# VectorE's scan reads its additive term from SBUF for 27 of 192 units, in a fused state-space and attention kernel

## The reference, cut to what matters

```
def step(h, inp):
    dt_t, B_t, C_t, x_t = inp
    h = jnp.exp(dt_t[:, :, None] * A) * h + (dt_t * x_t)[:, :, None] * B_t[:, None, :]
    y_t = jnp.einsum('ben,bn->be', h, C_t)
    return (h, y_t)
...
y = ys.transpose(1, 0, 2) + xr * D
y = y * jax.nn.silu(z)
return y @ W_out
```

## Time and profile before

| | |
|---|---|
| time, median of 3 runs (range) | 1211.03 us (1209.63 to 1213.32) |
| the profiled execution: its time, its span | 1210.56 us, 1208.8 us |
| DVE busy over the span | 931.2 us (77%) |
| POOL busy | 938.3 us (78%) |
| PE busy | 1055.9 us (87%) |
| ACT busy | 571.8 us (47%) |
| first read-out to last read-out of the recurrence | 58.2 to 756.6 us |

### The profile page before, as it was taken

One profiled execution on the slowest core, in us unless ns is written; L12 is line 12 of the kernel. 1 busy time (PEld: TensorE's weight loads), 2 busy tenths in 40 slices (PEclk: granted clock), 3 DMA queues, 4 the chain that ended last, 5 costly groups with the idle time before them and its releaser, 6 DMA issues. The chain is left out here.

```text
span 1208.8 us, 9466 instructions
## 1 busy us (share of the span) xinstructions
PE 1055.9 (87%) x3220; PEld 363.4 (30%) x3220; DVE 931.2 (77%) x608; ACT 571.8 (47%) x601; POOL 938.3 (78%) x375
## 2 busy tenths in 40 slices
PE   7789998789988998998878878499999999996675
PEld 2233333233332333333332223133333333332221
DVE  1499998679998999998989999400488695969871
ACT  5765867696778564866585634101111021010321
POOL 0089999989998979998999988300298977889880
PEclk9879999899999999998999999799999999998787
DMA  2244575535475545673546563253949586574402
GB/s 79 91 150 142 192 182 159 175 128 173 140 185 144 178 136 156 167 228 124 174 158 171 154 200 139 58 122 76 174 82 200 79 182 106 125 129 56 92 0 75
DMA packets 111041, 165.65 MB, mean 137 GB/s; under 512 B 63410, under 2 KB 76440, under 8 KB 110992
## 3 DMA queue, kind: packets, MB, share of 16 engines
q1 hardware_dynamic: 108880, 157.81, 50.0%
q10 hardware_dynamic: 2112, 7.23, 2.1%
HBM read 137.43 MB, written 11.23 MB: 123 GB/s over the span
## 5 line engine op out<-in xcount | busy, mean ns | idle before, releaser
L732 POOL TENSOR_TENSOR hc<-h,c_rep 128x1024 f32<-128x1024 f32 x192 | 449.6, 2354 | 99.0 <-DVE h L790 94.1
L790 DVE TENSOR_TENSOR_SCAN h<-a,bu 128x1024 f32<-128x1024 f32 x192 | 437.6, 2285 | 36.3 <-ACT bu L606 9.8
L422 PE MATMUL y_ps<-hc,ident 128*128 128x512 f32 x768 | 384.7, 626 | 3.5 <-POOL hc L732 1.9
L596 ACT ACTIVATE a<-dt,a_neg 128x1024 f32<-128x1024 f32 x192 | 216.7, 1143 | 136.5 <-DVE h L790 136.1
L1203 POOL TENSOR_TENSOR prod_p<-vw,at 128x3584 f32<-128x3584 f32 x18 | 130.2, 7236 | 122.9 <-DMA vw<-v_d 117.0
L777 DVE TENSOR_TENSOR bu<-bu,u 128x1024 f32<-128x1024 f32 x165 | 199.5, 1209 | 18.9 <-PE bu L400 18.9
L422 PEld LDWEIGHTS y_ps<-hc,ident 128*128 128x128 f32 x768 | 144.7, 197 | 213.5 <-issue 182.0
L1084 PE MATMUL sc_ps<-x,w_up 128*64 128x512 f32 x672 | 176.4, 602 | 0.0
L1084 PE MATMUL sc_ps<-x,w_low 96*64 96x512 f32 x672 | 175.7, 600 | 0.0
L400 PE MATMUL bu<-st,pick 96*128 96x512 bf16 (+1 forms) x438 | 103.1, 393 | 43.7 <-DVE h L790 40.2
L1154 ACT ACTIVATE sc<-sc_ps,rel 128x512 f32<-128x512 f32 x24 | 16.5, 687 | 246.8 <-PE sc_ps L1084 246.8
(11 more groups left out here) (126 smaller groups left out, 973.3 us busy)
## 6 DMA issues: line engine op xcount, KB each, us to landing
c_rep<-bc_d SPq DMA_DIRECT2D x128, 512.0 KB, 3.8
c_rep<-bc_d SPq DMA_DIRECT2D x128, 256.0 KB, 4.1
vw<-v_d SPq DMA_DIRECT2D x24, 532.0 KB, 9.5
x<-qk SPq DMA_DIRECT2D x66, 171.0 KB, 6.3
b_rep<-bc_d SPq DMA_DIRECT2D x17, 512.0 KB, 5.0
b_rep<-bc_d SPq DMA_DIRECT2D x20, 256.0 KB, 5.5
scores_d<-sc ACTq DMA_DIRECT2D x24, 196.0 KB
at<-scores_d SPq DMA_DIRECT2D x24, 196.0 KB, 5.1
```

What stands on the lines that cost most here:

```text
L422: mm = pe.matmul(y_ps[:, cols(th)], ident[:, :], hc[:, k % HC_RING, cols(th)], start=(n == 0 and d == 0), stop=(n == N_ST - 1))
L596: nc.scalar.activation(a[:, k % A_RING, :], dt[:, tile % 2, :], ACT.Exp, scale=a_neg[:, kind_of(tile), n:n + 1]).then_inc(exp_done, 1)
L732: nc.gpsimd.tensor_tensor(hc[:, k % HC_RING, :], h[:, k % H_RING, :], c_rep[:, k % C_RING, :], ALU.mult).then_inc(hc_done, 1)
L790: nc.vector.tensor_tensor_scan(scan_order(h[:, k % H_RING, :], d), scan_order(a[:, k % A_RING, :], d), scan_order(bu[:, k % 2, :], d), 0.0 ...
```

## The change

The 27 units of `POOL_UNITS` lose ACT's copy (`copy_b` and the semaphore `b_copied` are gone). Their scans read POOL's product where it stands, in `b_rep` in SBUF, and wait for `b_times_u`. The load that overwrites a buffer of `b_rep` waits for the scan that read it, no longer for the copy. The 165 other units are as before.

```diff
@@ SP, load_b @@
                 if i >= B_RING:
-                    sp.wait_ge(b_copied, i - B_RING + 1)
+                    sp.wait_ge(scanned, POOL_UNITS[i - B_RING] + 1)
                 replicate(b_rep, i % B_RING, k, 0, b_in[i % B_RING])
@@ ACT @@
-            def copy_b(k):
-
-                if k not in POOL_UNITS:
-                    return
-                i = POOL_UNITS.index(k)
-                act.wait_ge(b_times_u, i + 1)
-                act.wait_ge(scanned, k - 1)
-                nc.scalar.activation(bu[:, k % 2, :], b_rep[:, i % B_RING, :], ACT.Copy).then_inc(b_copied, 1)
@@
             for k in range(UNITS):
                 copy_y(k)
-                copy_b(k + 1)
                 decay(k + 2)
                 front(k)
@@ DVE, scan @@
                 if k in POOL_UNITS:
-                    dve.wait_ge(b_copied, POOL_UNITS.index(k) + 1)
+                    i = POOL_UNITS.index(k)
+                    dve.wait_ge(b_times_u, i + 1)
+                    term = b_rep[:, i % B_RING, :]
                 else:
                     dve.wait_ge(bu_done, products_before(k + 1))
+                    term = bu[:, k % 2, :]
                 if k >= H_RING:
                     dve.wait_ge(hc_done, k - H_RING + 1)
                 nc.vector.tensor_tensor_scan(
                     scan_order(h[:, k % H_RING, :], d), scan_order(a[:, k % A_RING, :], d),
-                    scan_order(bu[:, k % 2, :], d), 0.0, ALU.mult, ALU.add).then_inc(scanned, 1)
+                    scan_order(term, d), 0.0, ALU.mult, ALU.add).then_inc(scanned, 1)
```

More of the change, by code:

```diff
@@ L205, in mamba @@
         b_times_u = sem("b_times_u")
-        b_copied = sem("b_copied")
         block = ctx.enter_context(nc.Block())
```

## The result

The changed kernel takes 1269.02 us (median of 4 runs, 1267.12 to 1275.68) against 1212.17 us before: ratio 1.0481, interval 1.0438 to 1.0525, 57 us slower. The profiled execution took 1268.18 us with a span of 1266.4 us.

What follows compares the result with a forecast made beforehand. DVE and POOL together were taken to bound the recurrence, each with little slack. The terms 29.7 + 0.4 + 9 - 3 - 3 gave +33 us on 1210.56 us, 1243.6, forecast as 1244, range 1218 to 1274.

Steps and rivals of the forecast that it cites:

- the two bounds: Limits for exclusion in any order: at least +19 us (1230), and +58 (1269) if every POOL standstill arrives at the end.
- shared by halves: Rival: scan and POOL operation both run at half speed while they overlap, 59 less 3 us, 1268; chance 0.07.
- part 2: The scan's new wait for b_times_u and the load's new wait for the scan were to cost nothing.
- Alone the second operand costs hardly anything: The 27 scans' second SBUF operand, without interference, was to cost 13 ns each, 0.4 us in all.
- Exclusion, with the scan starting when POOL's operation in progress ends: The 27 scans meet POOL 94% of the time, waiting 1.10 us on average: +29.7 us; chance 0.66.
- POOL goes first: Last rival listed: DVE gets in only when POOL's queue runs dry, 3 us a scan, +81 us, 1290; chance 0.09.
- POOL loses 2.15 us a scan, 58 us in all: POOL was to stand still 2.15 us for each of the 27 scans, 1.05 us more than DVE loses each time.
- POOL's gaps swallow a part, the rest arrives as +9 us: POOL's loss beyond DVE's was to vanish in POOL's gaps; elsewhere DVE waits for late read-outs, 4 and 5 us.
- The copy's wait gives 3 us and ACT's freedom 3 more: Under exclusion, dropping the copy was to gain 3 us at unit 53 and 3 us from ACT's queue.
- The range leaves out no more than 0.2: The range 1218 to 1274 was set to leave out the first rival and most of the last.
- the first rival: No interference between the scans and POOL: the time falls by 9 us, to about 1202; chance 0.13.
- the second: Rival: a little interference, as much as dropping the copy gives back, within 0.3% of before, 1211; chance 0.05.

Runs made afterwards that it cites:

- the relief alone: Changed kernel, but the 27 scans read their half of bu in PSUM, where an older product stands, instead of b_rep: 1211.57 us, ratio 0.9991.
- its control: Kernel before, with POOL made to wait on its own last read-out and product near the 27 units: 1219.58 us, ratio 1.0053.
- slack units: Kernel before, with only units 51, 53, 65, 68, 80, 83, 97 and 99 reading the product in SBUF: 1235.51 us, ratio 1.0179.
- the gap runs: POOL waits on its own last operations near the 27 units: in the changed kernel 1253.32 us, in the kernel before 1219.58 us.
- the port alone: Kernel before, copy and its waits kept, with the 27 scans reading the product in b_rep in SBUF: 1270.51 us, ratio 1.0477.
- tight units: Kernel before, with only units 22, 36, 38, 46, 147, 153, 163 and 165 reading the product in SBUF: 1234.95 us, ratio 1.0177.
- the runs with 8 units: Two runs of the kernel before with the operand changed for 8 of the 27 units only: 1235.51 us and 1234.95 us.

## Why the prediction was right, and its size wrong

The direction and the exclusion were right, and 1269 lies at the upper of the two bounds (1230 and 1269). The forecast itself, 1244, was 25 us too low, since the rule of hand-over was wrong. The time alone would not have told the theories apart: the rival "shared by halves" gave 1268. The rows rule it out, since at unit 22 the scan keeps its 2.27 us while POOL's read-out beside it takes 4.25.

- *The waits cost nothing* (part 2): right; the run with the relief alone shows it at 0.9991.
- *Alone the second operand costs hardly anything*: right. The scans of units 83 and 99, with POOL idle or nearly so, took 2.28 us, and the ten that came first 2.27.
- *Exclusion, with the scan starting when POOL's operation in progress ends*: **this step failed.** Most waiting scans, 12 of 15, wait for POOL to run dry. The term that hangs on it, +29.7 us, measured 64.8. The rival "POOL goes first" had the mechanism, at a chance of 0.09 and a price too high (3 us a scan, measured 2.4, since 12 of 27 scans wait for nothing). Where gaps make the failed step true, the operand costs 34 us over its control, and the forecast had been +33. That the sums meet is in part luck: the mean wait was 1.46 us, not 1.10. The 1.10 took the scans as falling anywhere within a POOL operation, but 6 of the 15 that waited were released by the end of one (they began 0.13 us behind the end of the read-out that they needed, as unit 46 does in the earlier trace rows) and met the next one at its very start.
- *POOL loses 2.15 us a scan, 58 us in all*: nearly right. Thirteen operations blocked behind a scan lengthened by 1.9 to 2.0 us each, 25 us, and behind each of the 12 scans that waited for POOL to run dry it stood idle for some 2.23 us, 27 us: 52 us for 25 scans, and the other two met no POOL operation to speak of. That its busy and idle time together grew by 58.7 us is no proof of the 58: POOL's work is the same, so this is the growth of the stretch itself.
- *POOL's gaps swallow a part, the rest arrives as +9 us*: no. In the stretch with POOL's gaps the 8 slack units cost 20.7 us for 22 us waited. And the waits for read-outs, which were to bring those 9 us, did not come: POOL catches up while the scan waits, and a passed scan finds all read-outs done. DVE's waits for read-outs grew from 6.7 to 8.6 us only.
- *The copy's wait gives 3 us and ACT's freedom 3 more*: alone they give 1, within the noise. In the changed kernel DVE's idle time fell by 6.4 us, which is these terms' size, but only beside scans that waited 65 us.
- *The range leaves out no more than 0.2*: by its own chances it leaves out more. Its lower end, 1218, is above both the first rival (0.13) and the second (0.05), and its upper end below most of the last (0.09), together about 0.25.

In DVE's account of the recurrence, 64.8 of the 65.1 us that it is busy longer lie in these 27 scans; less 6.4 us of idle time, this is the 58.7 us that the recurrence grew by.

## What to carry to other kernels

A DVE scan with both inputs in SBUF, beside a GpSimd that works back to back on SBUF, mostly waits not for one operation but for GpSimd's whole line of ready ones. So price it by the length of that line, not by half an operation, and expect no help from GpSimd's gaps; only DVE's own idle time takes some of it up. One operand in PSUM avoided it altogether, whichever of the two it was, and the engine copy that puts it there can be cheap: here its removal was worth 1 to 2 us, not clear of noise. If two SBUF inputs can't be avoided, a GpSimd wait on its own last operation opens the line for a gap of 0.1 to 0.2 us each. Only the scan was tried here; that other DVE instructions with two SBUF inputs fare alike is not shown.

## What was not expected of the hardware

- The handing over depends on tenths of a us. With the next POOL operation starting 0.03 us ahead of the end of the last one the scan is passed over, with it starting 0.08 to 0.17 us behind that end, never. The times of POOL's operations are rough at this scale, but the gap runs bear the contrast out. In the changed kernel, though, 3 scans got in without such a gap. For two of them what POOL's next operation waited for had come only 0.14 and 0.16 us before (ACT's `mid`, below, which ends at 598.98 where POOL's read-out ends at 599.12; PE's sum at unit 153); for the third, unit 185, everything was there 0.9 us before. Other runs have more of that third kind: units 51 and 53 in the run with the slack units, 97 and 185 in the run with the port alone, each with POOL's next operation ready for about 1 us. At unit 22 of the run with the tight units it had been ready for as long, and the scan was passed over. What decides then stays open.

```profile
596.78 2.34 POOL L721 TENSOR_TENSOR hc<-h,c_rep 128x1024 f32<-128x1024 f32 x1
...
597.92 1.06 ACT L526 ACTIVATE mid<-dbc 32x1024 bf16<-32x1024 f32 x1
598.10 3.17 DVE L782 TENSOR_TENSOR_SCAN h<-a,b_rep 128x1024 f32<-128x1024 f32 x1
...
599.08 4.10 POOL L665 TENSOR_TENSOR st<-dbc,mid 32x1024 bf16<-32x1024 f32 x1
```

- The granted clock of PE, a mean over its two levels of 2.4 and 1.2 GHz, fell in the recurrence from 0.96 to 0.91, while PE's idle time rose from 81 to 115 us; its busy time for the same work rose from 617 to 642 us. No run tells how much of the 57 us that is. DVE's waits for PE did not grow (18.9 us before, 17.4 after), but the 3 us that the runs with 8 units lost where no unit was changed warn that it need not be nothing.
